# A two-layer cross-attention kernel: the short TensorE steps of a pair put in two groups, one head's transposes a block product ahead

## What is computed

```
K = rmsnorm(ctx @ Wk)        # 512 context rows per batch row; layer 0 has 32 latent rows besides
V = ctx @ Wv
S = Q @ K.T                  # layer 1 adds a mask
P = softmax(S)
O = P @ V                    # for each of 8 key/value heads, 4 query heads x 32 rows = 128 rows at once
x = x + O @ Wo
```

## Time and profile before

| what | us |
|---|---|
| median of 3 runs | 1540.71 |
| the profiled execution, whole | 1542.61 |
| its span (first to last instruction) | 1540.8 |
| TensorE busy | 1448.2 (94%) |
| VectorE busy | 1043.0 (68%) |
| ScalarE busy | 764.1 (50%) |
| GpSimd busy | 422.8 (27%) |
| the pairs of layer 0, V tile of pair 0 to V tile of pair 31 | 105.35 to 629.72 |
| the pairs of layer 1, the same | 859.74 to 1342.86 |

### The profile page before, as it was taken

One profiled execution on the slowest core, in us unless ns is written; L12 is line 12 of the kernel. 1 busy time (PEld: TensorE's weight loads), 2 busy tenths in 40 slices (PEclk: granted clock), 3 DMA queues, 4 the chain that ended last, 5 costly groups with the idle time before them and its releaser, 6 DMA issues.

```text
span 1540.8 us, 23740 instructions
## 1 busy us (share of the span) xinstructions
PE 1448.2 (94%) x7942; PEld 1191.0 (77%) x7942; DVE 1043.0 (68%) x1829; ACT 764.1 (50%) x1412; POOL 422.8 (27%) x574
## 2 busy tenths in 40 slices
PE   8988999996999999899999899999799999999998
PEld 6856777775888888779767688888688888777887
DVE  6776766776666666777767666666766666777766
ACT  5745555554445444655547344444444444463443
POOL 2555443344222222105126222222322222201000
PEclk9999999998999999999999999999899999999999
DMA  7453344354333433345434333335233333434242
GB/s 274 151 197 138 137 172 148 133 199 147 127 120 111 135 123 110 137 155 201 125 139 184 116 123 117 124 118 189 73 125 124 116 123 117 151 117 145 83 164 96
DMA packets 65516, 215.13 MB, mean 140 GB/s; under 512 B 16976, under 2 KB 21840, under 8 KB 58160
## 3 DMA queue, kind: packets, MB, share of 16 engines
q1 hardware_dynamic: 65424, 213.95, 40.7%
HBM read 180.76 MB, written 33.16 MB: 139 GB/s over the span
## 4 chain that ended last, share of the span: by engine, by line
PE 63%; DVE 16%; issue 9%; ACT 5%; DMA 4%; POOL 3%; SPq 0%; DVEq 0%; ACTq 0%; POOLq 0%
PE g_kbanks L54 9%; PE g_kbanks L56 8%; PE g_kbanks L55 8%; PE g_pobanks L1712 7%; PE g_ktbank L1725 4%; PE g_vbank L54 4%; PE g_vbank L55 4%; PE g_vbank L56 3%; PE g_pobanks L1700 3%; PE g_sbank L1687 2%; DVE c0a_nmax L1978 2%; DVE c1a_kn L2012 2%; PE g_pobanks L54 1%; PE g_sbank L54 1%; DVE c_cT_r L410 1%
## 5 line engine op out<-in xcount | busy, mean ns | idle before, releaser
L54 PE MATMUL g_kbanks<-c_wkv_r,c_cT_r 128*128 128x512 f32 x768 | 322.5, 420 | 16.3 <-ACT c0a_v L1899 5.0
L56 PE MATMUL g_kbanks<-c_wkv_r,c_cT_r 128*128 128x512 f32 x768 | 304.0, 396 | 0.0
L55 PE MATMUL g_kbanks<-c_wkv_r,c_cT_r 128*128 128x512 f32 x768 | 303.1, 395 | 0.0
L54 PEld LDWEIGHTS g_kbanks<-c_wkv_r,c_cT_r 128*128 128x128 f32 x768 | 146.1, 190 | 45.0 <-DVE c_wkv_r L212 5.3
L56 PEld LDWEIGHTS g_kbanks<-c_wkv_r,c_cT_r 128*128 128x128 f32 x768 | 145.4, 189 | 34.3
L55 PEld LDWEIGHTS g_kbanks<-c_wkv_r,c_cT_r 128*128 128x128 f32 x768 | 146.3, 190 | 21.4
L1608 POOL TENSOR_TENSOR c1a_ms<-c1a_ss,c_const 128x4 f32<-128x4 f32 x64 | 13.7, 214 | 372.0 <-DVE c1a_ss L2007 372.0
L54 PE MATMUL g_vbank<-c_wkv_r,c_cT_r 128*128 128x512 f32 x256 | 106.8, 417 | 0.6 <-DVE c0a_v L2061 0.6
L1608 POOL TENSOR_TENSOR c0a_ms<-c0a_ss,c_const 128x4 f32<-128x4 f32 x64 | 13.7, 214 | 335.8 <-DVE c0a_ss L2007 335.7
L1846 ACT ACTIVATE c1a_p<-c1a_sm,c1a_nmax 128x512 f32<-128x512 f32 x64 | 46.3, 723 | 120.0 <-DVE c1a_nmax L1983 120.0
L56 PE MATMUL g_vbank<-c_wkv_r,c_cT_r 128*128 128x512 f32 x256 | 101.0, 395 | 0.0
(11 more groups left out here) (536 smaller groups left out, 3796.6 us busy)
## 6 DMA issues: line engine op xcount, KB each, us to landing
c_cT_r<-ctx_split_dram SPq DMA_DIRECT2D x48, 1024.0 KB, 5.5
c_cT_r<-ctx_split_dram SPq DMA_DIRECT2D x48, 768.0 KB, 4.8
ctx_split_dram<-c_cT_r SPq DMA_DIRECT2D x16, 1792.0 KB, 6.4
c_wkv<-in_l_wo SPq DMA_DIRECT2D x16, 1024.0 KB, 4.9
g_stage<-in_l_wq SPq DMA_DIRECT2D x15, 1024.0 KB, 6.3
e_stage<-in_e_w SPq DMA_DIRECT2D x20, 768.0 KB, 4.3
c_wkv<-in_l_wkv SPq DMA_DIRECT2D x16, 512.0 KB, 6.6
c_cT<-in_ctx SPq DMA_DIRECT2D x32, 256.0 KB, 3.0
```

What stands on the lines that cost most here:

```text
L54: nc.tensor.matmul(out, a[0], b[1], start=start, stop=False, skip_group_check=reopen)
L55: nc.tensor.matmul(out, a[0], b[0], start=False, stop=False, skip_group_check=reopen)
L56: return nc.tensor.matmul(out, a[1], b[0], start=False, stop=stop, skip_group_check=reopen)
```

## The change

On TensorE a pair's short steps stand in two groups. The first lies between p2 and p6: p_transpose of one head, score of the next, kt of tile 2m-1, pv of the first head. The second lies between p7 and p4: score, kt of tile 2m, pv; its p_transpose stands one product ahead, between p5 and p7. So the heads come later by half a pair or more than before, and one head more is left for `finish`.

The rest follows from it. Probabilities, their transposes and layer 1's masked scores have one buffer instead of two; a new tile `keep` holds the two partial sums of V that ScalarE wrote to `v`; K of tile 2m+1 is copied out of its bank (`kb_kept`) and normalised in SBUF. `pt_copy` moves from VectorE to ScalarE; the latent columns' part moves to VectorE whole (`tail_heads`, three instructions) and is turned into the V bank or `y_bank` instead of the transposes' bank. The square root of tile 2m-1 moves to the start of GpSimd's next pair. At the turn T1 and T4 are differences on VectorE, T3 is made in the next pair, and the last two blocks are split there.

```diff
+    def turned_t1(self, dve):
+        dve.wait_ge(self.loaded[0], 32)
+        dve.wait_ge(self.loaded[2], 32)
+        self.quick_difference(self.low(self.T1), self.raw[:, self.SPARE, 0, :], self.low(self.B11))
+
+    def turned_t2(self, pool):
+        pool.wait_ge(self.loaded[3], 32)
+        pool.wait_ge(self.summed, 5)
+        self.difference(self.low(self.T2), self.raw[:, self.SPARE, 1, :], self.low(self.T1))
+
+    def turned_t4(self, dve):
+        dve.wait_ge(self.loaded[1], 32)
+        dve.wait_ge(self.summed, 6)
+        self.quick_difference(self.low(self.T4), self.low(self.B21), self.low(self.T2))
+
+    def turned_t3(self, pool):
+        pool.wait_ge(self.summed, 7)
+        self.difference(self.low(self.T3), self.raw[:, self.SPARE, 1, :], self.raw[:, self.SPARE, 0, :])
...
+    keep = s.sb("keep", [P, 2, UW])
+    sm = s.sb("sm", [P, CTX]) if mask is not None else None
     gate = s.sb("gate", [P, 1]) if mask is not None else None
     nmax = s.sb("nmax", [P, UNIT_H])
     rsum = s.sb("rsum", [P, UNIT_H])
     rinv = s.sb("rinv", [P, UNIT_H])
-    p = s.sb("p", [P, 2, KEYS])
-    pT = s.sb("pT", [P, 2, CT, P])
-    pTs = s.sb("pT_stack", [STACK, 2, P], F32R) if tail else None
+    p = s.sb("p", [P, KEYS])
+    pT = s.sb("pT", [P, CT, P])
+    pTs = s.sb("pT_stack", [STACK, P], F32R) if tail else None
...
+    def scored(u, par, side, second):
+
+        if second:
+            return UNIT_H * (u - 1) + 2 * side, u - 1, 1 - par, 2 * side
+        if side:
+            return UNIT_H * (u - 1) + 1, u - 1, 1 - par, 1
+        return UNIT_H * (u - 2) + 3, u - 2, par, 3
+
+    def summed_up(u, par, side, second):
+
+        if side:
+            return UNIT_H * (u - 1) + int(second), u - 1, 1 - par, int(second)
+        return UNIT_H * (u - 2) + 2 + int(second), u - 2, par, 2 + int(second)
...
         def quad(hf, b, par, cycle, u, side, m):
+            if is_at(m, PAIRS // 2):
+                pool.wait_ge(products, made(m - 1, "p4"))
+            if not is_at(m, 0):
+                root(2 * m - 1, 1)
+            if is_at(m, PAIRS // 2):
+                kvw.turned_t3(pool)
...
             product(side, context.A11, kvw.B11, x_bank, True).then_inc(products, 1)
             if is_at(m, 0):
                 border.turn(pe, 0)
-            if lags(u, side):
-                pv(a - 1, 1 - par if side else par, (2 * side - 1) % UNIT_H)
-            need(pe, k_normed, 2 * m)
             wait_weights(kvw.B21)
+            need(pe, kb_kept, m)
             product(side, context.A12, kvw.B21, y_bank, True).then_inc(products, 1)
             if is_at(m, 0):
                 border.turn(pe, 1)
             else:
-                kt(2 * m - 1, 1, a if on else 0)
+                p_transpose(summed_up(u, par, side, False)[0], va_added, m, zbank)
+                score(*scored(u, par, side, False))
+                kt(2 * m - 1, 1)
+                pv(*summed_up(u, par, side, False), loads)
             wait_weights(kvw.T2)
             pe.wait_ge(p1_kept, m + 1)
             product(side, context.S2, kvw.T2, x_bank, False).then_inc(products, 1)
@@ -1772,51 +1795,42 @@
             wait_weights(kvw.T1)
             need(pe, va_added, m)
             product(side, context.S1, kvw.T1, zbank, True).then_inc(products, 1)
-            if on:
-                if side == 0:
-                    wait_unit(u, par)
-                score(a, 1 - par, 2 * side)
+            p_transpose(summed_up(u, par, side, True)[0], ka_added, m + 1, y_bank)
             wait_weights(kvw.T3)
             pe.wait_ge(u2_kept, m + 1)
             product(side, context.S3, kvw.T3, x_bank, False).then_inc(products, 1)
-            if on:
-                kt(2 * m, 0, a)
-                score(a + 1, 1 - par, 2 * side + 1)
+            score(*scored(u, par, side, True))
+            kt(2 * m, 0)
+            pv(*summed_up(u, par, side, True), loads)
             wait_weights(kvw.T4)
             pe.wait_ge(u3_kept, m + 1)
             product(side, context.A22, kvw.T4, x_bank, False).then_inc(products, 1)
-            if on:
-                p_transpose(a, 2 * side, 2 * m + 1)
-            else:
-                kt(2 * m, 0, 0)
             wait_weights(kvw.B22)
             pe.wait_ge(vb_added, m + 1)
             product(side, context.S4, kvw.B22, zbank, False).then_inc(products, 1)
...
+        def pt_copy(a):
+            if not exists(a):
                 return
             act.wait_ge(pt_done, a + 1)
-            need(act, o_done, a - 1)
-            for row in range(2):
-                nc.scalar.activation(pTs[row * ROWS:(row + 1) * ROWS, k % 2, :],
-                                     ktbank[0:SEQ, 0:P], ACT.Copy).then_inc(pt_tail, 1)
+            need(act, o_done, a)
+            nc.scalar.activation(pT[:, :, :], ptbank[:, :].rearrange("p (t n) -> p t n", t=CT),
+                                 ACT.Copy).then_inc(pt_ready, 1)
...
-                place_k(2 * m - 1, 3 - 2 * side, par if side else 1 - par, u if side else u - 1)
+                pt_copy(summed_up(u, par, side, False)[0])
             act.wait_ge(ka_added, m + 1)
             square(2 * m, kn[:, 0, :])
+            if not is_at(m, 0):
+                place_k(2 * m - 1, 3 - 2 * side, par if side else 1 - par, u if side else u - 1)
+                exponential(x1, k1)
             act.wait_ge(products, made(m, "p6"))
-            need(act, o_done, UNIT_H * (u - 1))
-            nc.scalar.activation(v[:, par, 2 * side, :], x_bank, ACT.Copy).then_inc(u2_kept, 1)
+            need(act, va_added, m)
+            nc.scalar.activation(keep[:, 0, :], x_bank, ACT.Copy).then_inc(u2_kept, 1)
+            divide(x1, k1)
             if prepared(hf, m + 1):
                 for i in range(2):
                     context.make_hi(act, *following(hf, b, side), i)
             if last:
-                for i in range(2):
-                    out.make_hi(act, i)
-            if on:
-                exponential(a, 2 * side)
-            act.wait_ge(products, made(m, "p7"))
-            nc.scalar.activation(v[:, par, 2 * side + 1, :], x_bank, ACT.Copy).then_inc(u3_kept, 1)
-            if on:
-                divide(a, 2 * side)
-            place_k(2 * m, 2 * side, par, u)
-            if is_at(m, PAIRS // 2 - 1):
-                for n in range(3):
-                    kvw.turned_hi(act, n)
-            if last:
                 act.wait_ge(products, made(m, "p1"))
                 for i in range(2):
                     wo.make_hi(act, i)
-            if on:
-                exponential(a + 1, 2 * side + 1)
-                tail_heads(a, 2 * side)
+            if turning:
+                kvw.turned_hi(act, 0)
+            if turned:
+                kvw.turned_hi(act, 5)
+                kvw.turned_hi(act, 6)
+            pt_copy(summed_up(u, par, side, True)[0])
+            act.wait_ge(products, made(m, "p7"))
+            need(act, vb_added, m)
+            nc.scalar.activation(keep[:, 1, :], x_bank, ACT.Copy).then_inc(u3_kept, 1)
+            place_k(2 * m, 2 * side, par, u)
+            exponential(x2, k2)
+            if turning:
+                kvw.turned_hi(act, 1)
+            if last:
+                for i in range(2):
+                    out.make_hi(act, i)
             act.wait_ge(products, made(m, "p4"))
-            square(2 * m + 1, x_bank)
-            if on:
-                divide(a + 1, 2 * side + 1)
-            if is_at(m, PAIRS // 2 - 1):
-                act.wait_ge(products, made(m, "p3"))
-                for n in range(3, kvw.COUNT):
+            need(act, kt_done, 2 * m)
+            nc.scalar.activation(kn[:, 1, :], x_bank, ACT.Copy).then_inc(kb_kept, 1)
+            act.wait_ge(kb_kept, m + 1)
+            square(2 * m + 1, kn[:, 1, :])
+            divide(x2, k2)
+            if turning:
+                for n in range(2, 5):
                     kvw.turned_hi(act, n)
...
+        def tail_heads(a, bank):
+            if not tail or not exists(a):
+                return
+            dve.wait_ge(tail_turned, a + 1)
+            need(dve, o_done, a)
+            nc.vector.tensor_copy(pTs[0:ROWS, :], bank[0:SEQ, 0:P]).then_inc(tail_hi, 1)
+            nc.vector.tensor_copy(pTs[ROWS:2 * ROWS, :], bank[0:SEQ, 0:P])
+            dve.wait_ge(tail_hi, a + 1)
+            nc.vector.tensor_tensor(pTs[2 * ROWS:STACK, :], bank[0:SEQ, 0:P], as_f32(pTs[0:ROWS, :]),
+                                    ALU.subtract).then_inc(tail_ready, 1)
...
             late_split(2)
-            if lags(u, side):
-                pt_copy(a - 1, (2 * side - 1) % UNIT_H)
             if not is_at(m, 0):
-                need(dve, kt_done, 2 * m - 2)
-                normalise(2 * m - 1, 1, y_bank)
-            if lags(u, side):
-                if side:
-                    ot_place(a - 1, u - 1, 1)
-                else:
-                    ot_place(a - 1, u - 2, UNIT_H - 1)
+                normalise(2 * m - 1, 1)
+                tail_heads(summed_up(u, par, side, False)[0], zbank)
```

(68 more changed lines are left out.)

223 lines of the change are left out of this document (102 added, 121 removed).

## The result

Four runs of the changed kernel took 1528.02 to 1532.44 us, median 1529.79, beside 1540.56 to 1542.45 us before, median 1540.72. The ratio is 0.9928, 95% interval 0.9909 to 0.9947: 11 us faster. The forecast was 1486 us with a range from 1471 to 1513. The sign is right; the size is off by 44 us, and the time lies outside the range.

The account below looks back on a forecast made before the run. The prediction took TensorE's own order and waits as the bound (busy 94% of the span). Gains of 11.4, 4.3, 16.1, 13.8, 5.9 and 3 us, 54.5 in all, gave 1486.2 us, range 1471 to 1513.

Parts of the forecast that it names:

- The ends: First pairs and `finish`: 3 us gained (0 to 8); the last pairs of both layers: 5.9 us gained.
- The turn: Pairs 15 and 16: 39.4 us in layer 0, 37.6 in layer 1, 13.8 us gained together.
- The steady pair of layer 1: Plain pairs of layer 1: 0.44 us gained a pair, 11.4 us over 26 pairs.
- The new wait: Second group's p_transpose waits for ScalarE's division: 0.08 us, or 0.16 with drained array and overlap, in each pair.
- Part (b): Steady pair: fewer changes between fp32 and fp32r steps on TensorE, net gain 0.08 us.
- Layer 0: Pairs 17 to 30 gain 0.31 us each, 4.3 us; pairs 3 to 14 gain 1.34 us each, 16.1 us.
- Rival 1: Probability chain makes the second p_transpose wait 0.5 us in each pair, 30 us in all: 1516 us; chance 0.16.
- Rival 3: First group's kt waits for a late K tile; at 2.2 us late 78 us are lost: 1564 us; chance 0.05.
- Rival 4: TensorE's clock falls in the longer groups of short steps, 66 us over 60 pairs: 1552 us; chance 0.03.
- Rival 2: The turn and layer 0's first half don't gain, VectorE still having all low parts: 1506 us; chance 0.16.

Follow-up runs that it names:

- e1: The changed kernel with the products of `finish` in the order of the kernel before: 1484.03 us, ratio 0.9627.
- e2: The changed kernel with the output weights' halves 12 to 15 split one loop step earlier in `finish`: 1506.58 us, ratio 0.9773.
- e5: e1 with pair 15's split context in layer 0 stored behind the loads of the new weights instead of ahead: 1479.41 us, ratio 0.9591.
- e6: e1 with the second group's p_transpose back beside its score, behind p7: 1480.38 us, ratio 0.9598.
- e7: e1 with the first group's pv behind p6 instead of ahead of it: 1476.43 us, ratio 0.9571.
- e8: The kernel before the change, with one VectorE low part of the context moved behind the next pair's multiplication in layer 0's first half: 1530.17 us, ratio 0.9921.
- e11: e1 with two more GpSimd power operations ahead of the root of K tile 2m-1, in layer 0 alone: 1530.10 us, ratio 0.992.
- e9: e6 with kt ahead of the score in both groups: 1486.17 us, ratio 0.9639.
- e10: e5 with two VectorE low parts moved from the end of pair 15 into pair 16: 1472.73 us, ratio 0.955.

## Why the prediction was wrong

**The ends: the step that failed.** The prediction took "3 us for all of that (0 to 8)" for the first pairs and `finish`, on the argument that `finish` has one head more, which is the work that the first pairs lack. It counted work and looked at no order. The first pairs gave 10.1 us, `finish` took 45.8 (e1). With pair 0's 0.8 us the term came out at 36.5 us lost for 3 won: 39.5 of the 43 us of error in the span. The rest is layer 0's turn, 6.6 us short, and layer 0's pairs, 4.9 us better than forecast, with 2.1 us in smaller terms. The term was given one sentence, and the orders of ScalarE and VectorE there were never held against TensorE's. The rule of e2 could have been read from the diff: product `2j+4` of step j against halves split for `2j+3`. With `finish` in its old order the kernel takes 1484.0 us (e1), within 3 us of the 1486 forecast, but part of that is luck: the first pairs' 10.1 us and layer 0's 5 make up for what its turn did not give.

**The turn: half right.** Layer 1 came out at 37.87 us for 37.6 forecast, with one stall at kt (4.6 us) and one at p7 (1.5 us), as forecast. Layer 0 came out at 46.06 for 39.4. The sum was worked out for layer 1 and carried over; layer 0 has a store of 1792 KB just ahead of the weights' load, and ScalarE's copy of the transposes now stands behind that load. e5 gives back 4.9 of the 6.7 us; what is left stands beside kt's wait, 4.88 us there for 4 forecast, and the low clock (0.92 in e5's turn). I had not asked what is queued behind the instruction that waits.

**The steady pair of layer 1: right in mechanism and sum.** 0.42 us a pair for 0.44. The distance from p7's last matmul to kt was 0.46 us too long in the 14 second groups of pairs 17 to 30, as forecast, and this wait is gone. The first group's kt has 0.9 us to spare as forecast, but in every second pair only 0.5, because the multiplication beside a GpSimd instruction is longer; the prediction had 0.6 to 0.7 us for it in every pair. The new wait is 0.08 us and costs 0.11 to 0.13 (e6, e7) for 0.16. Part (b) was wrong in its parts, 0.11 and 0.09 us with opposite signs in place of 0.08 and 0.04, and small in its sum.

**Layer 0: right in mechanism.** The 1.03 us of its first half were VectorE's low part (e8 removes 0.89 of them); the 0.31 us for pairs 17 to 30 were 0.50. The trace before has what the sum left out: in 8 places of these pairs pv starts 0.40 to 0.58 us after the matmul ahead of it where the pace is 0.23, 2.35 us in all or 0.17 a pair, and in the changed kernel pv never waits there. No run tests it.

**Rivals.** Rival 1 named the right wait and a size that did not occur. Rival 3 did not occur in the change, but e11 and e9 show that its mechanism is real, 0.5 to 1.2 us away. Rival 4 fell: the granted clock of all plain stretches is 1.00, with groups of 2.4 us. Rival 2 was half true, in layer 0's turn. None of the rivals was about `finish`.

## What to carry to other kernels

When a pipeline's steady part is shifted by a step, hold the orders of all engines in its epilogue against one another product by product: an epilogue that was tuned for the old lag can take back the whole gain. Price a stall of several microseconds with the clock behind it, not by its bracket alone. And look for the wait that one misplaced instruction makes (e8, e5) before rearranging a schedule; here e5 and e10 gave 11 us for one DMA and two low parts moved.

## What the runs showed of the hardware

- The clock: behind three stalls of 3.95 and 4.12 us the granted clock was 0.50 for a whole product, 5.25 us of busy array. Idle time of 2.61 us ahead of kt in e10 left it at 1.00, while the 2.54 us ahead of the stretch in the earlier trace rows did not (0.58). It isn't a matter of the gap alone: behind 3.95 us in layer 1 the clock fell only after five matmuls, and behind almost the same wait, 3.89 us in e1 and 3.95 in e7, pv took 2.08 us in the one and 1.16 in the other, where it was the product behind pv that ran at the low clock.
- A change between fp32 and fp32r steps costs 0.02 us net, though single distances differ by 0.09 to 0.11.
- VectorE's multiplication of a K tile with both inputs in SBUF takes 0.69 us alone. Beside a GpSimd instruction it ended 0.55 us after that one's end: 1.78 us beside a subtraction (L1644), 1.08 beside a cast (L1641). VectorE, then GpSimd:

```profile
1266.56 1.08 DVE L2041 TENSOR_TENSOR c1a_kn<-c1a_kn,c1a_rstd 128x512 f32<-128x512 f32 x1 [0.87 <-POOL c1a_rstd L1630]
...
1271.26 1.78 DVE L2041 TENSOR_TENSOR c1a_kn<-c1a_kn,c1a_rstd 128x512 f32<-128x512 f32 x1 [0.64 <-POOL c1a_rstd L1630]
...
1281.27 0.69 DVE L2041 TENSOR_TENSOR c1a_kn<-c1a_kn,c1a_rstd 128x512 f32<-128x512 f32 x1 [0.87 <-POOL c1a_rstd L1630]
```

```profile
1266.48 0.61 POOL L1641 CAST c1a_q_hi<-c_qT 128x512 fp32r<-128x512 f32 x1
...
1271.19 1.30 POOL L1644 TENSOR_TENSOR c1a_q_lo<-c_qT,c1a_q_hi 128x512 fp32r<-128x512 f32 x1
```

The row of 1271.26 is K tile 2m, which lay in SBUF before the change too. The other two rows are tile 2m+1, which the change moved there. Before, it was read from PSUM, and it took 0.69 us beside the same cast, which ran from 1236.22 to 1236.83:

```profile
1236.37 0.69 DVE L2012 TENSOR_TENSOR c1a_kn<-g_kbanks,c1a_rstd 128x512 f32<-128x512 f32 x1
```

So the move costs 0.39 us of VectorE in every second pair. The GPSIMD Engine Reference of the Trainium skill says in its specifications that VectorE instructions with two SBUF inputs contend with GpSimd; by that rule the move of the K tile into SBUF has such a price, and the trace agrees. It stayed hidden in the changed kernel, since kt had 0.9 us to spare and kept 0.5, and it came out in e9.
